# Cross-attention with layer norm: two of the three score products of two heads stacked in the 128 rows of TensorE

## What is computed

```python
qh = split_heads(x @ Wq.T + bq); kh = split_heads(ctx @ Wk.T + bk); vh = split_heads(ctx @ Wv.T + bv)
scores = where(mask == 0, -1e9, einsum('bhqd,bhkd->bhqk', qh, kh) / sqrt(32))
e = exp(scores - max(scores)) * mask
probs = e / (sum(e) + 1e-9)
attn = einsum('bhqk,bhkd->bhqd', probs, vh) -> (B, S, 512)
y = attn @ Wo.T + bo + x
out = (y - mean(y)) / sqrt(var(y) + 1e-5) * ln_g + ln_b
```

## Time and profile before

| | us |
|---|---|
| median of 3 runs (lowest to highest) | 596.99 (595.14 to 597.56) |
| the profiled execution, its own time | 597.65 |
| its span in the trace | 595.9 |
| TensorE busy (matmuls) | 563.6 (95%) |
| VectorE busy | 528.8 (89%) |
| ScalarE busy | 503.9 (85%) |
| GpSimd busy | 436.8 (73%) |
| time of the packets of SP's DMA queue, share of 16 engines | 31.9% |

### The profile page before, as it was taken

How to read it: one execution, slowest core, us unless ns; L and a number is a source line. 1 busy time by engine, 2 the same in 40 slices (tenths; PEclk the granted TensorE clock), 3 DMA queues, 4 the chain that set the end, 5 groups by cost and what they waited for, 6 DMA issues and landing times.

```text
span 595.9 us, 15264 instructions
## 1 busy us (share of the span) xinstructions
PE 563.6 (95%) x5460; PEld 457.6 (77%) x5460; DVE 528.8 (89%) x803; ACT 503.9 (85%) x2284; POOL 436.8 (73%) x401
## 2 busy tenths in 40 slices
PE   3998698999999999999999999999999999998894
PEld 3887576878878787878878787878878787886673
DVE  4778989898989999998989999898989999799876
ACT  5389799999899898999889997999889997699421
POOL 3405944699677969799487986799587976697787
PEclk9999989999999999999999999999999999899899
DMA  8924320232336005430336031430336122301252
GB/s 303 340 100 140 134 71 3 71 94 76 100 106 231 3 0 177 179 102 20 116 125 225 8 112 49 178 100 19 107 110 215 44 76 86 107 19 56 51 198 106
DMA packets 36198, 64.91 MB, mean 109 GB/s; under 512 B 12443, under 2 KB 14491, under 8 KB 34075
## 3 DMA queue, kind: packets, MB, share of 16 engines
q1 hardware_dynamic: 35979, 63.94, 31.9%
q10 hardware_dynamic: 144, 0.00, 0.0%
HBM read 44.15 MB, written 19.46 MB: 107 GB/s over the span
## 4 chain that ended last, share of the span: by engine, by line
PE 90%; DVE 7%; issue 1%; DMA 1%; POOL 0%; DVEq 0%; ACT 0%; SPq 0%
PE qo_bank L437 30%; PE qo_bank L541 28%; PE s_bank L437 18%; PE av_bank L527 10%; PE av_bank L452 1%; PE av_bank L437 1%; DVE WoT_lo L823 1%; DVE TP L895 1%; PE s_bank L541 1%; DVE E L866 1%; DVE bn L918 1%; DMA E<-in_WkT 1%; DVE Y L933 1%; DVE qo_bank L912 0%; DVE neg_max L874 0%
## 5 line engine op out<-in xcount | busy, mean ns | idle before, releaser
L691 ACT ACTIVATE E<-E,neg_max 128x77 f32<-128x77 f32 x1024 | 354.0, 360 | 22.2 <-DVE neg_max L874 21.9
L691 ACT ACTIVATION_READ_ACCUMULATOR E<-E,neg_max 128x1 f32 x1024 | 204.6, 200 | 0.0
L1184 POOL TENSOR_TENSOR E<-E,inv_sum 128x1232 f32<-128x1232 f32 x64 | 145.4, 2280 | 37.4 <-DVE inv_sum L881 37.2
L866 DVE TENSOR_TENSOR E<-s_bank,mask_bias 128x616 f32<-128x616 f32 x128 | 101.4, 792 | 24.1 <-PE s_bank L437 22.7
L437 PE MATMUL s_bank<-Kd,QT_hi 128*128 128x308 f32 x512 | 112.5, 307 | 0.0
L874 DVE TENSOR_REDUCE neg_max<-E 128x8 f32<-128x624 f32 x128 | 99.7, 786 | 0.6
L895 DVE STREAM_TRANSPOSE TP<-E 128x1280 f32<-128x1280 f32 x64 | 95.1, 1496 | 0.7 <-POOL E L1184 0.4
L437 PE MATMUL s_bank<-Kd,QT_lo 128*128 128x308 f32 x256 | 81.0, 316 | 9.2 <-DVE E L866 9.2
L437 PEld LDWEIGHTS s_bank<-Kd,QT_hi 128*128 128x128 f32 x512 | 84.9, 189 | 4.4
L1202 POOL TENSOR_TENSOR Y<-Y,b_row 128x512 f32<-128x512 f32 x62 | 79.2, 1299 | 3.1 <-ACT Y L708 2.9
L1155 POOL TENSOR_TENSOR sum_eps<-rowsum,sum_eps_c 128x16 f32<-128x16 f32 x64 | 14.6, 227 | 87.9 <-ACT E L691 87.8
(11 more groups left out here) (71 smaller groups left out, 826.7 us busy)
## 6 DMA issues: line engine op xcount, KB each, us to landing
Y<-in_x SPq DMA_DIRECT2D x16, 1024.0 KB, 5.8
out_y<-Y SPq DMA_DIRECT2D x64, 256.0 KB, 2.1
xT_raw<-in_xT SPq DMA_DIRECT2D x15, 1024.0 KB, 5.8
Vp<-V_scratch SPq DMA_DIRECT2D x32, 96.0 KB, 2.2
K_scratch<-TP SPq DMA_DIRECT2D x1, 1232.0 KB, 4.7
xT_raw<-in_xT SPq DMA_DIRECT2D x2, 512.0 KB, 7.0
Y<-in_WqT SPq DMA_DIRECT2D x4, 256.0 KB, 9.4
TP<-in_WvT SPq DMA_DIRECT2D x4, 256.0 KB, 8.1
```

The source lines that it names most:

```text
L691: last = cp(e, e, ACT.Exp, bias=neg_max[:, t, h:h + 1], accum_out=rowsum[:, t, h:h + 1])
L866: tt(E[:, t, :, 0:SK].rearrange("p (g j) k -> p g j k", g=2), s_bank[:, :, 0:GK].rearrange("p g (j k) -> p g j k", j=HG), mask_bias[:, row ...
L1184: nc.gpsimd.tensor_tensor(out=e, in0=e, in1=inv.unsqueeze(2).broadcast_to((P, 2 * HH, SK)), op=ALU.mult).then_inc(probs_ready, 1)
```

## The change

**Scores.** The rounded query of two neighbouring heads (64 rows) is copied by DMA into a new tensor `QS` twice, into rows 0 to 63 and again into rows 64 to 127. `Kd` holds, for the second and third product, the rounded keys of those two heads in the one half of the rows and their rests in the other. One matmul of 154 columns (two heads x 77) over all 128 rows then adds both hi x hi and hi x lo for two heads. An S becomes, for each `gi`, one matmul of 308 columns (`QT_lo` x hi) and two of 154 columns. The number of matmuls stays at 6.

**Buffers.** `QT_hi` and `QT_lo` lose their double buffer; `QS` is single too. `Q_hi(u)` waits until the copy of the unit before has landed, `Q_lo(u)` and the copy wait until the S of the unit before that read the same half are done. The context's split moves from the Q buffers into those of `Wo`, so the split of `Wo` waits for V.

**Queue of SP.** New: `stack(u, ab)`, four transfers of 256 KB for each half unit. `load_K` issues 12 smaller transfers where it issued 4.

**Last block.** Its rows of x go to the space of `xT_raw`, its OUTs into the four `av_bank`s without a wait for a `qo_bank`, its statistics into a place of their own, and all four of its rows end with `finish_row`. Of block 14, rows k = 0 and 1 (before: 2 and 3) go into `s_bank`.

**Order.** All five lists are written anew.

```diff
-        QT_hi = sb("QT_hi", [P, 2, 2, PAIR], FP32R)
-        QT_lo = sb("QT_lo", [P, 2, 2, PAIR], FP32R)
+        QT_hi = sb("QT_hi", [P, 2, PAIR], FP32R)
+        QT_lo = sb("QT_lo", [P, 2, PAIR], FP32R)
+        QS = sb("QS", [P, 2, 2, PAIR], FP32R)
...
         def out_bank(o, k):
-            return s_bank[:, k - 2, :] if split_out(o) and k >= 2 else qo("OUT", o, k)[:, :]
+            if last_out(o):
+                return av_bank[:, k, :]
+            return s_bank[:, k, :] if split_out(o) and k < 2 else qo("OUT", o, k)[:, :]
...
+                elif b == NB - 1:
+                    sp.wait_ge(q_ps, 4 * NB)
...
+                K = K_dram if batch else K_raw
                 for j in range(HG):
                     rows = slice(DK * j, DK * j + DK)
-                    sp.dma_start(Kd[rows, h, :, j, :].bitcast(FP32),
-                                 (K_dram if batch else K_raw)[rows, C * h:C * h + C, batch, :]).then_inc(Kd_loaded[h], 16)
+                    sp.dma_start(Kd[rows, h, 0:2, j, :].bitcast(FP32),
+                                 K[rows, C * h:C * h + 2, batch, :]).then_inc(Kd_loaded[h], 16)
+                for s in range(2):
+                    for r in range(HG):
+                        j, part = 2 * s + r % 2, C * h + r // 2 * 2
+                        sp.dma_start(Kd[DK * r:DK * r + DK, h, 2:4, j, :].bitcast(FP32),
+                                     K[DK * j:DK * j + DK, part:part + 2, batch, :]).then_inc(Kd_loaded[h], 16)
+
+            def stack(u, ab):
+                if not has(u):
+                    return
+                sp.wait_ge(q_hi, 4 * u + 2 * ab + 2)
+                if u:
+                    sp.wait_ge(s_ps, T2 * (u - 1) + T * ab + T)
+                cols = slice(ab * ROWS, ab * ROWS + ROWS)
+                for s in range(2):
+                    for part in range(2):
+                        sp.dma_start(QS[P // 2 * part:P // 2 * part + P // 2, s, :, cols].bitcast(FP32),
+                                     QT_hi[P // 2 * s:P // 2 * s + P // 2, :, cols].bitcast(FP32)) \
+                            .then_inc(stacked[ab], 16)
...
                 if t % T == 0:
                     pe.wait_ge(q_ready, 4 * u + 2 * (t // T) + 2)
+                    pe.wait_ge(stacked[t // T], 64 * (u + 1))
...
                 for gi in range(2):
-                    kd_hi, kd_lo = (Kd[:, h, 2 * l + gi, :, :].rearrange("p j k -> p (j k)") for l in range(2))
-                    q_hi_, q_lo_ = (q[:, h, gi, t * P:t * P + P] for q in (QT_hi, QT_lo))
-                    last = accumulate(s_bank[:, gi, 0:GK], [(q_lo_, kd_hi), (q_hi_, kd_lo), (q_hi_, kd_hi)])
+                    kd_hi, kd_two = (Kd[:, h, 2 * l + gi, :, :].rearrange("p j k -> p (j k)") for l in range(2))
+                    rows = slice(t * P, t * P + P)
+                    mm(s_bank[:, gi, 0:GK], QT_lo[:, gi, rows], kd_hi, start=True, stop=False)
+                    for s in range(2):
+                        cols = slice(s * 2 * SK, s * 2 * SK + 2 * SK)
+                        last = mm(s_bank[:, gi, cols], QS[:, s, gi, rows], kd_two[:, cols], start=False, stop=(s == 1))
                 last.then_inc(s_ps, 1)
...
-                if u >= 2 and gi == 0:
-                    act.wait_ge(s_ps, T2 * (u - 2) + T * ab + T)
+                if u and gi == 0:
+                    act.wait_ge(stacked[ab], 64 * u)
...
+                if u and gi == 0:
+                    dve.wait_ge(s_ps, T2 * (u - 1) + T * ab + T)
```

The general slots of TensorE and of SP, and TensorE's last ones, after the change:

```diff
+                elif s == 17:
+                    OUT(12, 3), S(15, 2), S(15, 3), AV(14, 0), S(15, 4), AV(14, 1), S(15, 5)
+                elif s == 18:
+                    OUT(13, 0), S(15, 6), S(15, 7), OUT(13, 1), OUT(13, 2)
+                elif s == 19:
+                    OUT_first(14, 0), OUT_first(14, 1), OUT(13, 3), AV(15, 0), AV(15, 1)
+                elif s == 20:
+                    OUT_first(14, 2), OUT_first(14, 3), OUT(14, 0), OUT(14, 1), OUT(14, 2), OUT(14, 3)
+                    OUT(15, 0), OUT(15, 1), OUT(15, 2), OUT(15, 3)
                 elif s % 2 == 0:
+                    OUT(s - 5, 3), S(s - 2, 2), Q(s - 1, 0), S(s - 2, 3), AV(s - 3, 0), AV(s - 3, 1)
+                    Q(s - 1, 1), S(s - 2, 4), OUT(s - 4, 0), S(s - 2, 5), S(s - 2, 6), OUT(s - 4, 1)
+                    S(s - 2, 7), Q(s - 1, 2), OUT(s - 4, 2), S(s - 1, 0), Q(s - 1, 3), S(s - 1, 1)
                 else:
+                    OUT(s - 5, 3), S(s - 2, 2), Q(s - 1, 0), S(s - 2, 3), AV(s - 3, 0), S(s - 2, 4)
+                    AV(s - 3, 1), Q(s - 1, 1), S(s - 2, 5), OUT(s - 4, 0), S(s - 2, 6), OUT(s - 4, 1)
+                    S(s - 2, 7), Q(s - 1, 2), S(s - 1, 0), OUT(s - 4, 2), Q(s - 1, 3), S(s - 1, 1)
...
                 elif s % 2 == 0:
+                    next_V(s - 2), store(s - 6, 0), store(s - 6, 1), store(s - 6, 2), store(s - 6, 3)
+                    load_rows(s - 4), stack(s - 2, 1), stack(s - 1, 0)
                 else:
+                    next_xT(s - 1), store(s - 6, 0), store(s - 6, 1), store(s - 6, 2), store(s - 6, 3)
+                    next_xT(s), load_rows(s - 4), stack(s - 2, 1), stack(s - 1, 0), store(s - 5, 0)
+                    store(s - 5, 1), store(s - 5, 2), store(s - 5, 3)
```

More of the change, by code:

```diff
@@ L182, in xattn_program @@
         q_ready = sem("q_ready")
+        stacked = [sem(f"stacked{i}") for i in range(2)]
         s_ps = sem("s_ps")
@@ L216, in xattn_program, with last_out @@
                 free_places += [AT_PLACE[v, i] for i in range(T) for v in (u - 1, u)]
+        def last_out(o):
+            return o == NB - 1
         def own_finish(o, k):
[L219 to L224 removed]
@@ new lines, in own_finish @@
+            return last_out(o)
+        QO_TURN = ((("OUT", 5, 3), ("Q", 1, 0), ("Q", 1, 1), ("OUT", 4, 0), ("OUT", 4, 1),
+                    ("Q", 1, 2), ("OUT", 4, 2), ("Q", 1, 3)),
+                   (("OUT", 5, 3), ("Q", 1, 0), ("Q", 1, 1), ("OUT", 4, 0), ("OUT", 4, 1),
+                    ("Q", 1, 2), ("OUT", 4, 2), ("Q", 1, 3)))
+        QO_EDGES = {-3: (("Q", 0, 0), ("Q", 0, 1), ("Q", 0, 2), ("Q", 0, 3)),
+                    1: (("Q", 1, 0), ("Q", 1, 1)),
+                    2: (("Q", 1, 2), ("Q", 1, 3)),
+                    17: (("OUT", 12, 3),),
+                    18: (("OUT", 13, 0), ("OUT", 13, 1), ("OUT", 13, 2)),
+                    19: (("OUT", 13, 3),),
+                    20: (("OUT", 14, 2), ("OUT", 14, 3))}
@@ L388, in _ @@
                 if s == -3:
-                    next_xT(0), next_xT(1)
+                    next_xT(0), next_xT(1), load_K(0), stack(0, 0), stack(0, 1), later_loads()
+                elif s == -2:
+                    load_K(1)
                 elif s == -1:
-                    load_K(0), later_loads(), load_K(1), save_K()
+                    save_K(), save_V(0)
                 elif s == 0:
-                    save_V(0), load_V(0), load_V(1)
+                    next_xT(2)
+                elif s == 1:
+                    pass
@@ L558, in OUT @@
                     return
-                qo_free("OUT", o, k)
+                if not last_out(o):
+                    qo_free("OUT", o, k)
                 if o == 0 and k == 0:
@@ new lines, in _ @@
+                    turn(0, 3), Q_lo(1, 3), bias(1, 3), row_max(1, 2), row_max(1, 3), split_lo("o", 0)
+                    split_lo("o", 1), split_lo("o", 2), split_lo("o", 3), inverse(1, 0), bias(1, 4)
+                    row_max(1, 4), AT_lo_(0, 0), AT_lo_(0, 1), AT_lo_(0, 2), AT_lo_(0, 3), bias(1, 5)
+                    row_max(1, 5), bias(1, 6), Q_lo(2, 0), Q_lo(2, 1), bias(1, 7), inverse(1, 1)
+                    row_max(1, 6), row_max(1, 7), turn(1, 0), turn(1, 1), inverse(1, 2), bias(2, 0)
@@ L1095, in _ @@
                 elif s % 2 == 0:
-                    row_max(s - 2, 7), Q_lo(s - 1, 2), residual(s - 4, 1), stats(s - 4, 1), bias(s - 1, 0)
-                    aggregate(s - 4, 1), row_max(s - 1, 0), center(s - 4, 1), turn(s - 2, 1)
-                    inverse(s - 2, 3), Q_lo(s - 1, 3), bias(s - 1, 1), turn(s - 2, 2), turn(s - 2, 3)
-                    row_max(s - 1, 1), residual(s - 4, 2), residual(s - 4, 3), bias(s - 1, 2)
-                    stats(s - 4, 2), stats(s - 4, 3), row_max(s - 1, 2), bias(s - 1, 3), aggregate(s - 4, 2)
@@ L1101, in _ @@
-                    aggregate(s - 4, 3), inverse(s - 1, 0), center(s - 4, 2), center(s - 4, 3)
-                    row_max(s - 1, 3), bias(s - 1, 4), turn(s - 1, 0), row_max(s - 1, 4), bias(s - 1, 5)
-                    Q_lo(s, 0), AT_lo_(s - 2, 0), AT_lo_(s - 2, 1), AT_lo_(s - 2, 2), row_max(s - 1, 5)
-                    Q_lo(s, 1), residual(s - 3, 0), inverse(s - 1, 1), stats(s - 3, 0), bias(s - 1, 6)
-                    aggregate(s - 3, 0), row_max(s - 1, 6), center(s - 3, 0), AT_lo_(s - 2, 3)
@@ new lines, in _ @@
+                    bias(s - 1, 0), stats(s - 4, 2), aggregate(s - 4, 2), row_max(s - 1, 0)
+                    center(s - 4, 2), turn(s - 2, 2), bias(s - 1, 1), inverse(s - 2, 3), Q_lo(s - 1, 3)
```

(5 more changed lines are left out.)

756 lines of the change are left out of this document (344 added, 412 removed).

## The result

The changed kernel takes **672.48 us** (median of 4 runs, 669.95 to 675.12) against 597.27 (595.14 to 598.88) for the kernel before on the same chip: a ratio of 1.126, 95% interval 1.120 to 1.133. I had forecast 590.7 with a range of 577 to 602 and 0.16 for slower.

A forecast was written before the change was run, and what follows sets the result against it. TensorE was taken to bound the kernel from 120 to 480 us. From the profiled 597.65: - 13.5 + 6.0 + 3.5 - 2.3 = 591.35, with the runs' median 0.66 lower: 590.7 us, range 577 to 602.

The forecast's parts named there:

- What one S costs: TensorE's S matmuls: 0.72 us per S against 0.85 to 0.86, gaining 13.5 us over units 3 to 15.
- The first: Rival on S: weight loads don't bind, a 154-column matmul takes 0.07 us, total 577.4 us; chance 0.15.
- the last rival: Rival on S: loads cost 0.14 us or more, S stays at 0.86, total about 600 us; chance 0.05.
- The second: Rival on VectorE and ScalarE: nearly full, they take the whole gain, total 597 us; chance 0.17.
- (1): Neighbouring S(u, 5) and S(u, 6) in TensorE's even slots: the second waits, 1.0 us each, 6.0 us lost.
- (2): Copies before S(u, 4) in odd slots: late by 0 to 1.4 us, 0.7 taken, 3.5 us lost in five slots.
- third rival: Copies before S(u, 4) in odd slots at half the rate: 4.1 us late, 20.5 in all, total 607.7; chance 0.13.
- 3.1 + 3 x 2.7: Three megabytes in SP's queue in odd slots: fixed part plus three transfer times, 11.2 us at most.
- (3): SP's queue: extra transfers for copies and load_K at 0.47 us each, under 8 us a unit, costing nothing.
- The start: S(0, 0) waiting for its copy: cost between -1 and +3 us, 0 taken; nothing counted before 120 us.
- two signs that it was wrong: Over 15 us of TensorE copy waits at S(u, 4) in odd slots; first 120 us changing by over 3.
- The end: Last block: AV starts 1.1 us sooner, finish 1.2 us sooner; gain 2.3 us, between 0 and 5.

The follow-up runs named there:

- run 5: Kernel before, order and buffers untouched, second and third 308-column product of S become two of 154 columns, without copies: 583.12 us, ratio 0.976.
- run 1: Changed kernel without the copies, the 154-column matmuls reading QT_hi in place of QS: 597.8 us, ratio 1.001.
- run 16: Changed kernel with copies of an eighth of the bytes (64 columns of 512), TensorE still waiting for them: 606.89 us, ratio 1.017.
- run 13: Changed kernel, all waits kept, each copy's four 256 KB transfers running over all 128 rows instead of 64: 629.6 us, ratio 1.055.
- 14: Changed kernel, each copy's four 256 KB transfers over all 128 rows, TensorE waiting for none and reading QT_hi: 604.31 us, ratio 1.012.
- run 2: Changed kernel with all copies issued, but TensorE waits for none and its 154-column matmuls read QT_hi: 649.05 us, ratio 1.087.
- run 17: Changed kernel, copies not waited for by TensorE, each transfer's 64 rows being every second row instead of a half: 604.86 us, ratio 1.013.
- 6: Changed kernel without the copies' transfers, but with SP's two waits for them left in its list: 597.17 us, ratio 0.998.
- 10: Changed kernel, four transfers per copy with an eighth of the bytes, TensorE not waiting for them: 597.0 us, ratio 0.999.
- the row tiles: Kernel before, order kept, no copies, each 308-column S matmul split into two 64-row tiles of 154 columns: 612.35 us, ratio 1.025.

## Why the prediction was wrong

Two terms were far too small: the copies, 75 us where I had 3.5, and the new order, 14.7 us where I had 6.0 less 2.3. The runs one behind the other, each step a difference of medians (the medians of the kernel before differ by up to 1.3 us beside them):

| | us | step |
|---|---|---|
| kernel before | 597.3 | |
| short matmuls, old order (5) | 583.1 | -14.2 |
| new order and buffers (1) | 597.8 | +14.7 |
| waits for copies of an eighth of the bytes (16) | 606.9 | +9.1 |
| full bytes, over 128 rows (13) | 629.6 | +22.7 |
| over a half of the rows (the change) | 672.5 | +42.9 |

And by stretch of the profiled executions (us), divided at the first S of units 4 and 15:

| | to S(4, 0) | S(4, 0) to S(15, 0) | to the end |
|---|---|---|---|
| before | 149.8 | 374.0 | 72.1 |
| 5 | 148.7 | 360.5 | 71.3 |
| 1 | 155.5 | 374.2 | 65.8 |
| 14 | 154.9 | 380.8 | 67.2 |
| 16 | 163.2 | 373.8 | 66.0 |
| 13 | 166.8 | 390.4 | 69.7 |
| 2 | 165.8 | 410.2 | 70.1 |
| the change | 176.9 | 428.2 | 67.3 |

**What one S costs: right.** The timeline of an S of the changed kernel (start, length, what):

```profile
301.38 0.30 PE L551 MATMUL s_bank<-Kd,QT_lo 128*128 128x308 f32 x1
301.52 0.34 PE L554 MATMUL s_bank<-Kd,QS 128*128 128x154 f32 x2
301.70 0.35 PE L551 MATMUL s_bank<-Kd,QT_lo 128*128 128x308 f32 x1
301.88 0.34 PE L554 MATMUL s_bank<-Kd,QS 128*128 128x154 f32 x2
302.07 0.43 PE L481 MATMUL qo_bank<-xT_hi,WqT_lo 128*128 128x512 f32 x1
```

0.14 for the first 308 and 0.18 for the second, 0.18 and 0.19 for the pairs of 154: 0.69 us where I had 0.72, against 0.86. The size is right in part by luck: a 154 takes 0.09 on the mean, not 0.11, and a 308 behind short ones 0.18, not 0.14; the two misses nearly cancel. In run 5 a unit has 32.6 us (median), where I had said 32.7. Gain 14.2 where I had 13.5. The first and the last rival (0.07 a matmul; an S that stays at 0.86) are out. The second is out for the old order: VectorE and ScalarE at 95.0% did not hold TensorE up in run 5. For the new order it is not: without copies this comes to 597.8 us (run 1), and that rival had said 597.

**(1) S side by side: the stall right, what the new order gives back too small.** 0.89 us each, six of them 5.3 where I had 6.0. But I had summed only the wait that I saw in the list, and the new order gave back the whole gain by itself: 14.7 us between runs 5 and 1, 13.7 of them between S(4, 0) and S(15, 0). There TensorE of run 1 is idle for 10.4 us (374.2 - 363.8, read over this stretch), in run 5 for 0.9; besides the pairs it waits 0.7 to 1.0 us four times before a Q or AV and once before S(13, 5). What makes up the other 4.2 of the 13.7 us is not settled.

**(2) The copies late: the failed step.** I had "late by 0 to 1.4; I take 0.7", from 391 GB/s for loads from outside, in all 3.5 us. The copies cost 74.7 us (the change against run 1), 25.6 of them as waits at S(u, 4) in the five odd slots. Three errors are in it.
- *The rate.* A copy with 64 rows of one half at both ends moves at about half the rate: 137 to 218 GB/s against 348 to 430, landing in 4.9 us against 2.5 (the change, run 13). My third rival had this price for another reason ("both sides of the copy are in the core's memory", which is so over 128 rows too, at 348 to 430 GB/s), and its sum comes near what happened in the slot: it said TensorE ready 9.8 us after the loads are freed and the third megabyte in 13.9, and 307.80 - 298.04 is 9.76, 312.52 - 298.04 is 14.5. It said 20.5 us for five slots; there are 25.6. I gave it 0.13, and took "an empty queue for most of the slot" as evidence against. The Trainium skill (SBUF — State Buffer, "Door 1: The DMA port swizzle") states that rows 0 to 63 reach only 8 of the 16 ports, with 196 GB/s for 1 MiB against 328 over 128 rows. The changed kernel's 137 to 218 and run 17 agree with it. My sum took loads over 128 rows for the price of a copy over 64.
- *Three megabytes in a row.* In run 13, at full rate, S(7, 4) still waits 3.4 us, and the five odd slots 2.7, 3.4, 2.2, 2.3 and 3.0: 13.7 in place of 3.5. From the first issue to the S it took 292.19 - 279.01 = 13.2 us there, not at most 11.2. Which term of 3.1 + 3 x 2.7 is too small, no run separates. SP's queue and the chain of run 13:

```profile
279.01 0.34 SPq L286 DMA_DIRECT2D xT_raw<-in_xT  x1
280.02 0.39 SPq L305 DMA_DIRECT2D Y<-in_x  x1
280.51 2.47 SPq L346 DMA_DIRECT2D QS<-QT_hi  x4
```

```profile
288.76 3.43 issue
292.19 0.60 PE s_bank L550
```

- *What else is in the queue.* I costed only who waits for the copy. The copies also hold up `xT` and `rows`: run 2 has 51 us with no product waiting for a copy, and there TensorE waits up to 3.5 us before AVs and 2.7 before Qs.

That nothing is late in the even slots came true: in the changed kernel no S(u, 4) of an even unit waits, nor an S(u, 0) from unit 3 on.

**(3) "Nothing" for SP: half right.** Issue and waits cost nothing (runs 6, 10), though four issues took 2.7 to 3.7 us, not 1.9. The "48% of 16 engines" was a total from bytes; it came to 52.3%, and the total did not show that transfers of this one queue come in order and have to come in time.

**The start: wrong.** I took 0 for S(0, 0) (measured +2.9, within the bounds) and nothing for the rest of the first 120 us, since "its work is not the bound". But the copy is on the path there: TensorE stands 5.8 us before S(1, 0) and 6.5 before S(2, 0), and the mean clock of these two stretches of 40 us is 0.79 and 0.76. SP's queue (start, length, what):

```profile
57.90 4.23 SPq L358 DMA_DIRECT2D Vp<-V_scratch  x8
62.65 3.53 SPq L346 DMA_DIRECT2D QS<-QT_hi  x4
...
73.60 21.20 SPq L373 DMA_DIRECT2D V_scratch<-V_st  x22
94.84 1.06 SPq L305 DMA_DIRECT2D Y<-in_x  x2
96.01 14.97 SPq L346 DMA_DIRECT2D QS<-QT_hi  x8
```

The copy for S(1, 0) goes out behind eight V loads, that for S(2, 0) behind 22 stores of V and two megabytes of rows; S(2, 0) starts at 108.81. Up to S(4, 0) the changed kernel loses 27.1 us: 5.7 by order (run 1), 11.3 by copies at full rate that are waited for (13), 10.1 by the half rows. Of the 11.3 us, 7.7 are there with hardly any bytes (run 16): there it is the place in the queue, not the rate. The prediction had named two signs that it was wrong, over 15 us of waits at S(u, 4) and a change of over 3 us in the first 120; both came.

**No term for the clock: wrong.** The nine stalls of 3.0 to 7.1 us all have a stretch at 1.2 GHz with them. With the others that is some 33 us, more than all the waits before S(u, 4) in the odd slots. The third rival had no such term either, nor the delay of the loads, and its 607.7 us is far too little.

**The end: right.** From the end of the last S to the end of the kernel: 43.6 us, before 46.5. A gain of 2.9, where I had 2.3. AV(15) starts at the end of the last transpose:

```profile
637.27 3.16 DVE L914 STREAM_TRANSPOSE TP<-E 128x1280 f32<-128x1280 f32 x2
```

```profile
640.61 3.94 PE av_bank L575 x172
```

**Is there a better version?** None of the runs that leave nothing out came under 597: the change with reordered transfers is at 668, the row tiles at 612. Run 5's 583 is what short matmuls reach in the old order with nothing that brings the stacked query. Heads interleaved row by row (every second row one pair of heads) should give copies the full rate; run 17 copied even rows to even and odd to odd only, and no run had a correct `QS` in this form. By run 13 it would end near 630 in this order, an estimate. Copies in the old order, with the double buffers, were not run either.
